# Third block of the next batch's layer-1 values copied out of PSUM ahead of the second pair of leaky passes of layer 2

## The reference, cut to what matters

```
xl   = x @ W                                  # "values"
e    = leaky_relu(a_src . xl[s] + a_dst . xl[d], 0.2)
e    = where(edge, e, -large)
attn = softmax(e)                             # over one side of the 512 x 512 matrix
out  = attn @ xl
```

## Time and profile before

| | |
|---|---|
| three runs, median | 949.05 us (948.87 to 951.0) |
| the profiled execution, its own time | 949.35 us |
| its span in the trace | 947.1 us |
| PE busy | 876.1 us (92%) |
| DVE busy | 753.7 us (80%) |
| ACT busy | 686.9 us (73%) |
| POOL busy | 257.2 us (27%) |

### The profile page before, as it was taken

The page is one execution under the profiler, slowest core; times in us unless marked ns, Lnnn a source line. Parts: engine busy times, 40 slices in busy tenths (PEclk is TensorE's granted clock), DMA queues, the critical chain, the costliest instruction groups (busy, mean ns, idle before and its releaser), DMA issues.

```text
span 947.1 us, 17311 instructions
## 1 busy us (share of the span) xinstructions
PE 876.1 (92%) x6220; PEld 815.5 (86%) x6220; DVE 753.7 (80%) x1908; ACT 686.9 (73%) x1274; POOL 257.2 (27%) x244
## 2 busy tenths in 40 slices
PE   5777889999999999999999999999999999999887
PEld 3676879998998989899898989989898998989775
DVE  6757687878888887888888788888878888887666
ACT  2566858778686887868688786868878686887653
POOL 1001001124231342423133242313324231331512
PEclk9897989999999999999999999999999999999999
DMA  7403030301203040120303013030301201000001
GB/s 200 128 1 90 1 89 1 87 4 34 79 19 94 1 108 5 34 79 21 93 1 109 4 35 78 22 91 1 112 2 35 77 24 23 1 24 1 23 1 67
DMA packets 62747, 45.03 MB, mean 48 GB/s; under 512 B 35780, under 2 KB 54340, under 8 KB 62664
## 3 DMA queue, kind: packets, MB, share of 16 engines
q1 hardware_dynamic: 62664, 43.93, 16.5%
HBM read 27.14 MB, written 8.39 MB: 38 GB/s over the span
## 4 chain that ended last, share of the span: by engine, by line
PE 35%; DVE 31%; ACT 24%; issue 8%; POOL 0%; DMA 0%; DVEq 0%; SPq 0%; POOLq 0%; ACTq 0%
DVE junk L888 10%; PE bU L530 7%; PE bU L509 6%; PE bG L602 6%; PE bG L616 6%; ACT att L720 6%; ACT att L705 6%; ACT x L732 5%; DVE y_lo L925 3%; DVE att L939 3%; PE bB L469 3%; DVE low L901 3%; DVE y L913 3%; ACT att L724 2%; DVE stats L978 2%
## 5 line engine op out<-in xcount | busy, mean ns | idle before, releaser
L509 PE MATMUL bU<-val,att 128*128 128x129 f32 x2048 | 249.5, 275 | 3.6 <-DVE att L939 3.6
L888 DVE CUSTOM_DVE_ANT_0 junk<-mask_t,bA,val 128x512 bf16<-128x512 bf16 x320 | 219.8, 743 | 35.5 <-PE bA L469 33.0
L509 PEld LDWEIGHTS bU<-val,att 128*128 128x128 f32 x2048 | 241.4, 192 | 6.0 <-issue 3.6
L939 DVE SCALAR_TENSOR_TENSOR att<-mask_n,att 128x2048 f32<-128x2048 bf16 x78 | 178.8, 2293 | 81.4 <-ACT att L720 81.0
L705 ACT ACTIVATE att<-bB,val 128x512 f32<-128x512 f32 x320 | 203.0, 708 | 3.1 <-PE bB L469 3.1
L720 ACT ACTIVATE att<-att 128x2048 f32<-128x2048 f32 x78 | 151.5, 1942 | 0.6
L772 ACT COPY val<-bG 128x524 f32<-128x524 f32 x64 | 38.7, 605 | 104.3 <-PE bG L616 104.3
L520 PE MATMUL bU<-val,att 128*128 128x257 f32 x480 | 109.8, 381 | 1.9 <-DVE att L935 1.2
L530 PE MATMUL bU<-val3s,att 128*128 128x256 f32 x480 | 109.2, 381 | 1.7 <-DVE res L969 0.2
L732 ACT ACTIVATE x<-bU,zinv 128x128 f32<-128x128 f32 x256 | 73.4, 375 | 47.6 <-DVE zinv L919 47.6
L380 POOL TENSOR_SCALAR var_eps<-moments 128x4 f32<-128x4 f32 x29 | 5.7, 195 | 368.0 <-DVE moments L981 368.0
(11 more groups left out here) (116 smaller groups left out, 1628.7 us busy)
## 6 DMA issues: line engine op xcount, KB each, us to landing
adj_in<-in_adj_dram SPq DMA_DIRECT2D x16, 1024.0 KB, 5.7
x_in<-in_x_dram SPq DMA_DIRECT2D x16, 512.0 KB, 6.7
out_dram<-act SPq DMA_DIRECT2D x14, 512.0 KB, 2.9
mask_t<-mask_n SPq DMA_TRANSPOSE x64, 2.5
att<-in_L_gnn_W_dram SPq DMA_DIRECT2D x4, 128.0 KB, 3.2
att<-in_L_gnn_W_dram SPq DMA_DIRECT2D x1, 512.0 KB, 7.6
out_dram<-x_in SPq DMA_DIRECT2D x1, 512.0 KB, 3.0
w<-in_L_gnn_W_dram SPq DMA_DIRECT2D x1, 256.0 KB, 7.2
```

Of the source, the lines that this page charges most:

```text
L509: ins = nc.tensor.matmul(to[:, (d % 2) * FX:(d % 2 + 1) * FX], p[:, s, d * P:(d + 1) * P], val1[u.batch % 2][:, s, u.index // 2, values], ...
L888: nc.vector.tensor_tensor_reduce(junk[:, b] if u.row else att[u.slot % 3][:, b], mask_t[u.batch % 4][:, b], bA[:], 1.0, a_col(u, b) if u.r ...
L939: nc.vector.scalar_tensor_tensor(flat(p), mask_n[u.batch % 3][:, 0:NB * N], BIG, flat(p), ALU.add, ALU.min)\
```

## The change

One call of ACT's list moves: the copy of block 2 of the next batch's values stands ahead of leaky passes 2 and 3 of the slot, no longer behind them. The other engines' lists are the same, row for row, and so are all tiles, waits and sizes.

```diff
                 if older:
                     normalize(older)
+                if pos == 5 and batch:
+                    values_1_out(n + 1, 2)
                 if this:
                     leaky(this, (2, 3))
                 if pos == 2 and batch:
@@
                 if pos == 4 and third:
                     values_3_out(n - 2, (0, 1))
-                if pos == 5 and batch:
-                    values_1_out(n + 1, 2)
                 if this:
                     exps(this)
```

## The result

| | before | after |
|---|---|---|
| runs | 20 | 20 |
| median us | 950.99 (948.85 to 952.63) | 952.5 (951.26 to 955.0) |
| ratio | 1 | 1.0021, 95% interval 1.0011 to 1.003 |
| span of the profiled execution | 947.1 | 949.7 |

The changed kernel is slower by 0.21%, 2.0 us, with an interval from 1.0 to 2.9 us; the two medians differ by 1.5 us. That is less than the 2.8 us which I had named as what a measurement can tell, but with 20 runs on each side the interval excludes no change. The same program varies by 3.7 to 3.8 us between launches, before and after, and not evenly. The 20 runs before fall into three groups, around 949.2 (8 runs), 951.0 (6) and 952.5 us (6); those after around 951.7 (10), 953.4 (8) and 955.0 (2). Group against group the change costs 2.3 to 2.5 us; the medians say less because they fall between groups that are differently filled.

What follows compares the result with a forecast made beforehand. The prediction took the chain through ACT's exponential and DVE, not PE, as the bound: 13 x 0.11 + (0 to 0.11) = 1.4 to 1.5 us on the median of 949.05 gave 950.5 us, range 948.6 to 952.6.

Steps and rivals of the forecast that it cites:

- What bounds this stretch: Position 5: the chain runs through ACT's exponential to DVE, not PE; 10.3 us of PE waits give back 0 us.
- The exponential's term: Position 5 on ACT: exponential directly behind its leaky pass ends 0.12 us later; 0.11 taken, ends 0 and 0.24.
- PE's lead: PE 0.73 us early from L613, cut to some 0.6 at layer 2's attention and 0.2 at the bB transposes.
- ACT's wait for the reciprocals: ACT at 503.08, behind block 3's copy: its wait for DVE grows from 0.54 to about 0.95 us.
- L613 without idle time: PE, first matmul of a values block: waits for the copy fall from 13.1 us to about 2.8, 17 to 4 times.
- the wait for `b_t`: PE at the bB transposes, 506.42: b_t ready only at 506.21, so PE's lead is cut to 0.2 us.
- Period n = 2: Position 5 of n = 2: no slack seen, counted as 0 to 0.11 us later.
- rival D: Copy's new place on ACT: copy could not run if block 2 were not ready; judged ready, no chance given.
- The sum: All changed periods: 13 x 0.11 plus 0 to 0.11, 1.4 to 1.5 us slower.
- The chances: Whole kernel: forecast 0.75, within 0.3% of no change 0.87, faster 0.05, slower 0.08.
- Within 0.3%: Whole kernel: change stays inside 2.8 us, which a measurement cannot tell from no change; chance 0.87.
- The clock rival: PE before 150 us: low-clock stretch lasts one 4 us window more, 2 us extra, 952.6 us in all; chance 0.08.

Runs made afterwards that it cites:

- Experiment 3: Changed kernel with eight more 128x128 transposes on PE at the end of position 5 of periods 1 to 14; 1.002 of before.
- experiment 4: Against the kernel before: copy of block 2 moved the other way, behind the exponential and directly ahead of block 3's copy; 985.17 us, 1.0375.
- experiment 2: Against the changed kernel: copy of block 2 one leaky pass later, between the two leaky passes; 1.0017 of before.
- 8: Changed kernel with the high part of y moved between the leaky passes and the exponential of position 5; 959.25 us, 1.0085 of before.
- Experiment 1: Changed kernel, but period n = 2 keeps the order of before; 1.0014 of before.
- experiment 7: Changed kernel with DVE's reciprocals of the third head ahead of the second layer norm's statistics; 940.2 us, 0.9895 of before.
- 5: Against the kernel before: PE makes block 2 at the end of position 4, ACT copies it ahead of normalize; 946.61 us, 0.9962.
- 6: Kernel before, ACT and PE order kept, with DVE's reciprocals of the third head ahead of the second layer norm's statistics; 931.51 us, 0.9802.

## Why the prediction was right or wrong

- *What bounds this stretch.* Right: the chain runs through ACT's exponential and DVE, and PE's waits of 10.3 us gave back nothing. Experiment 3 shows it for the part behind block 3. It holds in this direction only: experiment 4 makes PE later, and there it costs.
- *The exponential's term.* Right in cause and size: 0.12 worked out, 0.11 taken, 0.13 measured in each steady period. I had no reason to round down; the rows gave 0.12. Experiments 2, 4 and 8 show the cause.
- *PE's lead.* The outcome came as written, the steps mostly: ACT's wait for the reciprocals 0.97 us (0.95 said), L613 without idle time, the lead 0.62 us at L520 (0.6 said). I had put it at 0.73 at L613 by adding the transposes' full 0.60 us; L613 follows 0.36 us after their start, and it was 0.96. One wait I had not named: the second half of L520 waits 0.4 us a period for ACT's L732 and cuts the lead to 0.25 us; the wait for `b_t` then leaves 0.13 (0.2 said).
- *Period n = 2.* This is the step that failed. I counted it with 0 to 0.11 us and it cost 0.67. I had the earlier trace rows before me, in which PE's L613 of n = 2 has no idle time. That row says that PE was behind ACT there, and I read from it only that nothing could be won. In rival D I asked whether block 2 is ready at the copy's new place, answered it from one steady period, and gave it no chance. The answer is right for that period, by 1.0 us (block 2 done at 494.67, ACT there at 495.71), though not for the reason given: the transposes at 496.30 had not begun by then. In n = 2 block 2 is not ready, as the two rows of the kernel before show: 0.44 us of waiting, with the two leaky passes and the exponential behind it. Experiment 1 takes this wait away, experiment 2 most of it, and experiment 7 has it in every period, with the cost to match each time.
- *The sum.* 1.45 us forecast, 2.36 in the trace, 2.0 (1.0 to 2.9) by the runs. The difference to the trace is 0.6 from n = 2 and 0.3 from 13 periods of 0.13 against 0.11. The interval of the runs alone would not tell 1.45 from 2.36; the traces and the groups of runs do.
- *The chances.* "Within 0.3%" came true by size, but I had treated it as the same as no change, and 20 runs on each side told 0.2% from none. My steps led to slower, and slower is what was measured; the chance of 0.87 for no change hid it, and that step failed as well. The median of 952.5 lies just inside the range, near its upper end. Where it lies there is in part chance: of its 3.5 us over the forecast's base of 949.05, a median of three runs, 1.9 come from the runs of before, whose median is 950.99 here.
- *The clock rival.* Did not occur: 10.2 us of low clock in n = 1 and 6.8 in n = 2, before and after. It did add to experiment 4, and it spoils the L944 distance of n = 2 in the experiments where the stretch is shorter (1, 5, 6 and 7, 3.4 us each) or missing (8).

## What to carry to other kernels

A copy that stands between a producer and its consumer on one engine hides a little of the consumer's start; moving it out cost 0.13 us at each place here. Before an instruction is moved ahead of others on an engine that works in order, compare, in every phase of the program, the ramp too, the time at which its input is ready with the time at which the engine reaches the new place; if the input is late, all that was passed will wait. A missing wait on the far side is a hint of this: where PE had no idle time for the copy (n = 2), PE was the late one. And to shorten a period follow the chain of waits to the longest wait on it, not the busiest engine to its gaps: removing 10 us of waits of the engine at 92% was worth nothing, moving one pair of reciprocals was worth 19 us.

## What the runs showed of the hardware that I had not expected

A pause of 2.7 us on TensorE in each period (experiment 4) was followed by a stretch of 3.4 us at 1.2 GHz in 10 of 12 periods and by none in the two others with the same pause; it doubled the loss.

Launches of one program differ by 3.7 us, in groups 1.5 to 1.9 us apart, and in the traces the first 36 us differ by up to 4.5 us (L944 of period 0 at 31.66 to 36.18), more than the whole effect that was to be measured. The traces show where: of the four blocks of values that PE makes in the set-up, between 15 and 31 us, the L613 that opens a block takes 0.56 us in some and 0.36 in the others. One slow block goes with L944 at 31.7 to 32.0 us (before, after, experiment 7), two with 33.3 to 33.5 (2, 3, 5, 8), three with 34.8 (1, 4) and four with 36.2 (6). The products L616 of a slow block take 0.42 us instead of 0.28, as they do from 132 to 136 us, where the granted clock is 0.50. But the profile gives the granted clock of this early stretch as 1.00, with one slow block and with four, so the cause is not shown. That the groups of launches are these steps is likely by their size, but not shown.
